# Causal attention in equal steps: a long row's rest and a short row share one of 17 steps of a head pair

## The chip, the cores and the metric

The kernel runs on one core of a Trainium2 chip. The metric is the device time of one execution in microseconds (us), as the median of several runs. One execution was also profiled; its trace gives the rows below. Engines: PE is TensorE's matmul, PEld its weight load, DVE is VectorE, ACT is ScalarE, POOL is GpSimd, SP is SyncE, whose queue issues all DMA transfers of this kernel in program order.

## The reference

A sandwich layer on x of 2 x 2048 x 1024 float32: layer norm, causal self-attention with 16 heads of 64, layer norm of its output and residual; then layer norm, a gated expert FFN of low rank, layer norm and residual.

```python
scores = jnp.einsum('bqhd,bkhd->bhqk', q, k) * inv_sqrt_hd
causal = jnp.triu(jnp.ones((S, S), dtype=bool), k=1)
scores = jnp.where(causal[None, None, :, :], -jnp.inf, scores)
probs = jax.nn.softmax(scores, axis=-1)
attn = jnp.einsum('bhqk,bkhd->bqhd', probs, v).reshape(B, S, D)
return attn @ wo.T + bo
...
x = x + _layernorm(_L0_attn_ref(_layernorm(x), wq, bq, wk, bk, wv, bv, wo, bo))
x = x + _layernorm(_L0_ffn_ref(_layernorm(x), ...))
```

## The kernel before, in words

All matmuls run on float16 high and low halves: three products (low x high, high x low, high x high) stand for one float32 product.

The attention phase goes over 16 head pairs (a batch and two neighbouring heads each; pairs 0 to 7 are batch 0). In a pair the 2048 queries are 16 row tiles of 128 ("rows"), row t against t + 1 key blocks of 128. A long row (t from 8 to 15) is cut in a first part of 8 blocks and a rest of t - 7 blocks, whose results are rescaled to a common maximum and added; a short row (t from 0 to 7) is one part of t + 1 blocks. A round is one long and one short row, `(15, 0)`, `(14, 1)` and so on, in three steps: first part, rest, short row. So a pair has 8 rounds and 24 steps of 1 to 8 blocks. A step has one task for each of the two heads.

What each engine does for a task:
- PE, `scores`: 6 matmuls for each piece of up to 512 key columns (both heads of a pair at once, on 64 rows of the array each) into one of three PSUM tiles `s_ps`. It waits until the exponential of the step before's first head has read its tile.
- DVE, `row_max`: adds the mask to the diagonal block, takes the row maximum, makes the exponential's bias.
- ACT, `exponentials`: the exponential into `probs` (ring of 24 blocks), then a copy to float16 into `hl` (ring of 40 blocks).
- POOL, `probs_low`: the low half into `hl`.
- SP, `transpose_probs`: a DMA transpose of both halves into `pt` (ring of 40 blocks); before it can be issued, the task that held its place must have been multiplied (`pv_done`).
- PE, `times_v`: 3 matmuls of 65 columns for each block into `o_ps`.

The order is written by hand: in step i of pair p every engine runs its function `body`. PE issues the scores of step i + 3 (`LAG`), then a share of a projection unit of the next pair (`project`; 12 units a pair, for q, k and v in four chunks of tokens each, two steps for each unit), then the products with V of step i. DVE reads out a finished round (`output_read`, `output_sum`), does `row_max` of step i + 3, evacuates a finished unit (`unit_full`), splits the weights of a coming pair in halves (`split_weight`, placed by `SPLITS`). ACT and POOL go alike. In pairs 0 to 6 the layer norm of batch 1 is made in the second step of each round (`NORM_STEPS`), and in pairs 6 and 7 its 16 tiles are transposed from DRAM into `arena` (`TURN_STEPS`: pair 6 steps 10 to 22, pair 7 steps 0 to 16, every second one). After four rounds the output rows are split in halves and stored (`rows_high`, `rows_low`, `store_rows`).

The last pair has no projection beside it. In its step 0 SP loads four blocks of the output projection's weights (L382) and all eleven other inputs of the finish (L384); the further four blocks (L387) follow in steps 5 to 8. ACT, DVE and POOL centre and split these weights (`wo_sum`, `center_wo`, `wo_high`, `wo_low`).

The finish phase (a block of its own, with a barrier ahead of it) goes over 32 tiles of 128 tokens: output projection of 48 matmuls (L1143 to L1145), norms, FFN.

Of the kernel before, what the change touches and what calls it, by code (L numbers as in the profile page):

```python
# [12 lines left out]
P = 128  # L13
B, S, D, H = 2, 2048, 1024, 16
HD = D // H
# [43 lines left out]


STEPS = rounds(range(QT // 2))
FIRST_STEPS = rounds(reversed(range(QT // 2)))
steps_of = lambda p: STEPS if p else FIRST_STEPS
NSTEP = len(STEPS)
N_ROUND = NSTEP // PER_ROUND
# [8 lines left out]
TASK_BLOCKS = [nb for p in range(PAIRS) for t, k0, nb, acc in steps_of(p) for h in range(2)]  # L74


def ring(capacity):

    at, before, live, pos = [], [], [], 0
    for n, nb in enumerate(TASK_BLOCKS):  # L80
# [28 lines left out]
STEPS_PER_UNIT = NSTEP // N_UNIT  # L109


last_step = lambda kind, m: STEPS_PER_UNIT * (1 + max(u for u, (n, c) in enumerate(UNITS[kind]) if n == m)) - 1
# [4 lines left out]
SPLITS["last"] = {}  # L117

# [3 lines left out]
FREE_STEPS = [(p, i) for p in range(PAIRS) for i in range(1, NSTEP, PER_ROUND)][1:]  # L122
# [10 lines left out]
TURN_STEPS = {"pre": {10 + 2 * i: i for i in range(7)}, "turn": {2 * i: 7 + i for i in range(9)}}  # L133
# [11 lines left out]
def units_ending(kind, i):  # L145
    return [i // STEPS_PER_UNIT] if UNITS[kind] and i >= 0 and i % STEPS_PER_UNIT == STEPS_PER_UNIT - 1 else []


def attend_phase(nc, x, w_pairs, mask_in, xn_scratch, o_scratch, arena, fin):
    with ExitStack() as ctx:  # L150
        sb = lambda name, shape, dt: ctx.enter_context(nc.sbuf_tensor(name, shape, dt))
        psum = lambda name: ctx.enter_context(nc.psum_tensor(name, [P, 512], F32))
# [38 lines left out]
        s_ps = [ctx.enter_context(nc.psum_tensor(f"s_ps{i}", [P, CHUNK * P], F32)) for i in range(S_RING)]  # L191
        o_ps, u_ps = psum("o_ps"), psum("u_ps")
# [100 lines left out]

        def probs_of(n):
            return probs[:, P_AT[n] * P:(P_AT[n] + TASK_BLOCKS[n]) * P]
# [19 lines left out]
        def _(sp):  # L315
# [23 lines left out]
            def store_rows(p, half):  # L339
# [3 lines left out]
                for which in range(2):  # L343
                    first = min(steps_of(p)[PER_ROUND * r + 2 * which][0] for r in range(4 * half, 4 * half + 4))
# [4 lines left out]
            def body(p, kind):  # L349
                for i in range(NSTEP):  # L350
# [6 lines left out]
                    for tile in norm_tiles(p, i - 1, 2):  # L357
# [15 lines left out]
                    if i == 14:  # L373
# [14 lines left out]
                    if kind == "last" and i == 20:  # L388
# [29 lines left out]
        def _(pe):  # L418
            def scores(p, i):
                t, k0, nb, acc = steps_of(p)[i]  # L420
                n = NTASK * p + 2 * i
                pe.wait_ge(unit_lo_done, units_before(p, [("q", t // 4)] + [("k", c) for c in range((k0 + nb + 3) // 4)]))
                if n >= S_RING - 1:
                    pe.wait_ge(exp_done, n + 2 - S_RING)
                rows, qk = slice(t * P, (t + 1) * P), nat[p % 2]
                q_hi, q_lo, k_hi, k_lo = range(4)
                for at in range(0, nb * P, 512):
                    end = min(nb * P, at + 512)
                    keys = slice(k0 * P + at, k0 * P + end)
                    for q, k in ((q_lo, k_hi), (q_hi, k_lo), (q_hi, k_hi)):  # L430
                        for h in range(2):
# [75 lines left out]
        def _(dve):  # L507
# [53 lines left out]
            def row_max(p, i):  # L561
# [8 lines left out]
                for h in range(2):  # L570
                    n = NTASK * p + 2 * i + h
                    if diagonal:
                        dve.wait_ge(mask_done, masked + h + 1)
# [955 lines left out]
```

## Time and profile before

| | |
|---|---|
| median of 3 runs | 2527.53 us (2524.58 to 2529.49) |
| the profiled execution | 2525.55 us |
| its span, first to last instruction | 2523.8 us |
| before the first product with V | 116.4 us |
| pairs 0 to 14 | 116.4 to 1922.7 us |
| last pair, to the last product with V | 1922.7 to 2057.8 us |
| finish | 2057.8 to 2523.8 us |
| mean granted TensorE clock | 0.968 |

A share of busy time over the span mixes these stages. The bounds of the pairs are the starts of their first product with V in the trace. How to read a row is said at its group; "idle before us <-releaser" is the time an engine sat idle before these instructions, and what ended it.

### The profile page before, as it was taken

How to read it: one execution, taken by the hardware profiler on the slowest of the kernel's cores; microseconds unless marked ns; L12 is line 12 of the kernel's file. 1: busy time of each engine (PE TensorE's matmuls, PEld its weight loads, DVE VectorE, ACT ScalarE, POOL GpSimd, SP SyncE). 2: the span in 40 equal slices, each digit the busy share in tenths (PEclk: the TensorE clock that was granted, in tenths of full speed). 3: DMA queues.
4: the chain of work that ended last, by engine and by line, in shares of the span. 5: the costliest groups of instructions: out<-in, count | busy, mean ns of one | idle time of the engine just before them, and what ended most of it. 6: DMA issues, size and time to landing. Idle time of an engine off the chain costs nothing. (4 is left out here: it accounts for less than half of the span.)

```text
span 2523.8 us, 71940 instructions
## 1 busy us (share of the span) xinstructions
PE 2313.6 (92%) x28626; PEld 1451.6 (58%) x28626; DVE 1734.3 (69%) x4154; ACT 1782.1 (71%) x2579; POOL 1714.0 (68%) x1519
## 2 busy tenths in 40 slices
PE   4899999999999997899999999999997559999995
PEld 2466666575757655556675757666664334544452
DVE  8577877787777755567666776767665635777776
ACT  3477877777877866577778777877777835666664
POOL 4488888888878876678888788888887832222221
PEclk9999999999999999999999999999998779999997
DMA  9699999999999999999999999999999975666663
GB/s 240 128 199 192 202 191 194 199 194 189 202 192 199 189 185 188 194 167 193 173 184 183 171 184 178 190 169 189 169 173 193 174 147 134 167 153 159 161 164 84
DMA packets 1433645, 450.16 MB, mean 178 GB/s; under 512 B 1410240, under 2 KB 1411536, under 8 KB 1433312
## 3 DMA queue, kind: packets, MB, share of 16 engines
q1 hardware_dynamic: 1433312, 445.57, 95.7%
q8 instruction: 228, 3.74, 0.6%
q14 instruction: 105, 0.86, 0.1%
HBM read 67.95 MB, written 41.94 MB: 44 GB/s over the span
## 5 line engine op out<-in xcount | busy, mean ns | idle before, releaser
L848 POOL TENSOR_TENSOR hl<-probs,hl 128x1024 f16<-128x1024 f32 (+7 forms) x768 | 1229.3, 1612 | 366.3 <-ACT hl L731 365.5
L726 ACT ACTIVATE probs<-s_ps,exp_bias 128x1024 f32<-128x1024 f32 (+7 forms) x768 | 655.6, 854 | 386.3 <-DVE exp_bias L577 382.3
L574 DVE TENSOR_REDUCE neg_max<-s_ps 128x1 f32<-128x1024 f32 (+7 forms) x768 | 694.6, 904 | 68.9 <-PE s_ps L432 68.8
L731 ACT ACTIVATE hl<-probs 128x1024 f16<-128x1024 f32 (+7 forms) x768 | 620.5, 808 | 47.8 <-DMA pt<-hl 24.1
L450 PE MATMUL o_ps<-v,pt 128*128 128x65 f16 x4352 | 451.1, 194 | 60.4 <-DMA pt<-hl 50.7
L432 PE MATMUL s_ps<-nat 64*128 64x512 f16 (+3 forms) x3840 | 433.6, 354 | 65.2 <-ACT probs L726 60.3
L450 PEld LDWEIGHTS o_ps<-v,pt 128*128 128x128 f16 x4352 | 405.0, 97 | 107.6 <-issue 40.4
L451 PE MATMUL o_ps<-v,pt 128*128 128x65 f16 x4352 | 451.3, 195 | 0.0
L452 PE MATMUL o_ps<-v,pt 128*128 128x65 f16 x4352 | 449.4, 193 | 0.0
L479 PE MATMUL u_ps<-arena,w 128*128 128x512 f16 x1008 | 389.8, 387 | 40.2 <-DMA arena<-hl 35.3
L451 PEld LDWEIGHTS o_ps<-v,pt 128*128 128x128 f16 x4352 | 404.3, 98 | 27.8 <-issue 0.3
L452 PEld LDWEIGHTS o_ps<-v,pt 128*128 128x128 f16 x4352 | 405.0, 99 | 0.0
L480 PE MATMUL u_ps<-arena,w 128*128 128x512 f16 x1008 | 386.8, 384 | 0.0
L481 PE MATMUL u_ps<-arena,w 128*128 128x512 f16 x1008 | 386.4, 383 | 0.0
L475 PE MATMUL u_ps<-w,arena 128*128 128x128 f16 x1984 | 340.2, 220 | 0.7 <-DVE full L558 0.7
L476 PE MATMUL u_ps<-w,arena 128*128 128x128 f16 x1984 | 338.9, 219 | 0.0
L477 PE MATMUL u_ps<-w,arena 128*128 128x128 f16 x1984 | 338.9, 219 | 0.0
L569 DVE TENSOR_TENSOR s_ps<-s_ps,mask 128x128 f32<-128x128 f32 x512 | 126.5, 292 | 285.6 <-PE s_ps L432 285.1
L432 PEld LDWEIGHTS s_ps<-nat 64*128 64x128 f16 x3840 | 161.3, 95 | 211.1 <-issue 76.4
L479 PEld LDWEIGHTS u_ps<-arena,w 128*128 128x128 f16 x1008 | 99.0, 98 | 212.6 <-issue 115.8
L475 PEld LDWEIGHTS u_ps<-w,arena 128*128 128x128 f16 x1984 | 194.0, 98 | 38.3 <-issue 36.8
L1143 PE MATMUL proj_ps<-arena,w 128*128 128x512 f16 x512 | 195.0, 381 | 7.8 <-PEq L150 7.8
(150 smaller groups left out, 3690.4 us busy)
## 6 DMA issues: line engine op xcount, KB each, us to landing
w_raw<-in_w_pairs SPq DMA_DIRECT2D x48, 576.0 KB, 4.7
o_scratch<-o_hl SPq DMA_DIRECT2D x128, 128.0 KB, 2.6
out<-result SPq DMA_DIRECT2D x32, 512.0 KB, 2.9
x_in<-in_x SPq DMA_DIRECT2D x27, 512.0 KB, 5.1
pt<-hl SPq DMA_TRANSPOSE x768, 4.5
nat<-in_x SPq DMA_DIRECT2D x16, 512.0 KB, 4.8
xn_scratch<-xn SPq DMA_DIRECT2D x16, 512.0 KB, 4.2
xn<-in_x SPq DMA_DIRECT2D x11, 512.0 KB, 3.9
```

Source lines behind the costliest of these rows:

```text
L432: mm = nc.tensor.matmul(s_ps[(n + h) % S_RING][:, at:end], qk[HEADS[h], q, rows], qk[HEADS[h], k, keys], start=(q == q_lo), stop=(q == q_h ...
L450: nc.tensor.matmul(dst, lo, v_hi, start=(first and k == 0), stop=False)
L451: nc.tensor.matmul(dst, hi, v_lo, start=False, stop=False)
L452: mm = nc.tensor.matmul(dst, hi, v_hi, start=False, stop=(last and k == nb - 1))
L475: nc.tensor.matmul(dst, xt[:, 1, k, toks], hi[:, k, :], start=first, stop=False)
L479: nc.tensor.matmul(bank, lo[:, k, :], xt[:, 0, k, toks], start=first, stop=False)
L480: nc.tensor.matmul(bank, hi[:, k, :], xt[:, 1, k, toks], start=False, stop=False)
L481: mm = nc.tensor.matmul(bank, hi[:, k, :], xt[:, 0, k, toks], start=False, stop=last)
L574: nc.vector.tensor_reduce(neg_max[:, r, acc, h:h + 1], s_ps[n % S_RING][:, 0:nb * P], AX_X, ALU.max, negate=True).then_inc(max_done, 1)
L726: nc.scalar.activation(probs_of(n), s_ps[n % S_RING][:, 0:nb * P], ACT.Exp, bias=exp_bias[:, r, acc, h:h + 1], scale=SOFTMAX_SCALE).then_i ...
L731: nc.scalar.activation(hl_of(n, 0), probs_of(n), ACT.Copy).then_inc(p_hi_done, 1)
L848: nc.gpsimd.tensor_tensor(hl_of(n, 1), probs_of(n), hl_of(n, 0), ALU.subtract).then_inc(p_lo_done, 1)
```

## The change

The rounds are paired otherwise, so that a long row's rest and the short row of its round make 8 blocks together: `(14, 0)` has a rest of 7 and a short row of 1, `(8, 6)` of 1 and 7. They share one step, with one task for each head; only `(15, 7)` keeps three steps. A pair has 17 steps of 8 blocks each. In a shared step masks, maxima, biases and exponentials are made part by part; copy, low half, transpose and products with V run over the whole task. The place of a short row in the output scratch follows a table (`slot_of`).

Projection units take one or two steps each (`UNIT_STEPS`), the splits and the transposes of x have new steps, norm work stands in the step that closes a round. In the last pair the loads are dealt out over steps 0 to 6, two small matrices are laid out by partition on the host (a transfer of long rows), and the output projection of tile 0 (`project_half`) is issued at the end of the attention block, ahead of the barrier; PSUM tiles are shared by both phases for that.

```diff
-PER_ROUND = 3
-def rounds(order):
-    steps = []
-    for i in order:
-        t_long, t_short = QT - 1 - i, i
-        steps += [(t_long, 0, CHUNK, 0), (t_long, CHUNK, t_long + 1 - CHUNK, 1), (t_short, 0, t_short + 1, 2)]
-    return steps
+ROUNDS = [(14, 0), (13, 1), (12, 2), (15, 7), (11, 3), (10, 4), (9, 5), (8, 6)]
+FIRST_ROUNDS = [(8, 6), (9, 5), (10, 4), (11, 3), (12, 2), (13, 1), (14, 0), (15, 7)]
+SHORT_SLOTS = [3, 4, 5, 6, 0, 1, 2, 7]
+slot_of = lambda t: t if t >= CHUNK else SHORT_SLOTS.index(t)
+Step = namedtuple("Step", "round parts blocks opens closes")
+def steps(rows):
+    out = []
+    for r, (t_long, t_short) in enumerate(rows):
+        first, rest, short = (t_long, 0, CHUNK, 0), (t_long, CHUNK, t_long + 1 - CHUNK, 1), (t_short, 0, t_short + 1, 2)
+        shared = [[rest, short]] if rest[2] + short[2] <= CHUNK else [[rest], [short]]
+        tasks = [[first]] + shared
+        out += [Step(r, parts, sum(part[2] for part in parts), i == 0, i == len(tasks) - 1)
+                for i, parts in enumerate(tasks)]
+    return out
...
-STEPS_PER_UNIT = NSTEP // N_UNIT
+UNIT_STEPS = {"first": [1, 1, 2, 2, 1, 1, 1, 2, 1, 2, 1, 2], "mid": [1, 1, 1, 2, 1, 2, 1, 2, 1, 2, 1, 2],
+              "pre": [1, 1, 1, 2, 1, 1, 1, 2, 2, 1, 2, 2], "turn": [1, 1, 1, 2, 1, 1, 1, 2, 2, 1, 2, 2], "last": []}
-SPLITS = {kind: {4: "q", last_step(kind, "k") + 1: "k",
-                 max(last_step(kind, "k") + 4, last_step(kind, "v") + 1): "v"} for kind in ("mid", "pre", "turn")}
-SPLITS["first"] = {1: "v", 5: "q"} | {i: m for i, m in SPLITS["mid"].items() if m != "q"}
+SPLITS = {"mid": {3: "q", 6: "k", 14: "v"}, "pre": {3: "q", 13: "k", 16: "v"}, "turn": {3: "q", 13: "k", 16: "v"}}
+SPLITS["first"] = {1: "v", 4: "q", 7: "k", 14: "v"}
-FREE_STEPS = [(p, i) for p in range(PAIRS) for i in range(1, NSTEP, PER_ROUND)][1:]
+FREE_STEPS = [(p, i) for p in range(PAIRS) for i, step in enumerate(steps_of(p)) if step.closes][1:]
-TURN_STEPS = {"pre": {10 + 2 * i: i for i in range(7)}, "turn": {2 * i: 7 + i for i in range(9)}}
+TURN_STEPS = {"pre": {i: n for n, i in enumerate((6, 8, 9, 11, 12, 14, 15))},
+              "turn": {i: 7 + n for n, i in enumerate((0, 1, 3, 4, 5, 7, 8, 9, 10))}}
...
-                        for k in range(4):
-                            sp.dma_start(wo_raw[k], fin["w_view"][k]).then_inc(wo_loaded[k], 16)
-                        for tile, source in fin["loads"]:
+                    if kind == "last" and i < 4:
+                        sp.dma_start(wo_raw[i], fin["w_view"][i]).then_inc(wo_loaded[i], 16)
+                    if kind == "last" and i >= 1:
+                        for tile, source in fin["loads"][2 * i - 2:2 * i]:
                             sp.dma_start(tile, source).then_inc(fin_loaded, 16)
...
             def exponentials(p, i, h):
...
+                at = 0
+                for t, k0, nb, acc in step.parts:
+                    cols = slice(at, at + nb * P)
+                    last = nc.scalar.activation(probs_of(n)[:, cols], s_ps[n % S_RING][:, cols], ACT.Exp,
+                                                bias=exp_bias[:, step.round, acc, h:h + 1], scale=SOFTMAX_SCALE)
+                    at += nb * P
+                last.then_inc(exp_done, 1)
...
             pairs(body)
+            pe.wait_ge(exp_done, NTASK * PAIRS)
+            pe.wait_ge(wo_lo_done, KT)
+            pe.wait_ge(fin["ot_loaded"][0], 16)
+            for h in range(2):
+                project_half(nc, fin, 0, h)
```

## Rows read from the trace of the kernel before

**Rows 1.** The page: span, and busy time of each engine over the span.

```profile
span 2523.8 us, 71940 instructions
...
PE 2313.6 (92%) x28626; PEld 1451.6 (58%) x28626; DVE 1734.3 (69%) x4154; ACT 1782.1 (71%) x2579; POOL 1714.0 (68%) x1519
```

**Rows 2.** Busy time by stretch: pairs 0, 7, 10, 14, 15, and the finish.

```profile
core 0: us, PE busy (x) PEld busy (x) DVE busy (x) ACT busy (x) POOL busy (x), PEclk, DMA share, GB/s
...
116.40:236.80 120.40, 115.36 (x1633) 76.15 (x1632) 92.48 (x208) 93.46 (x132) 99.09 (x76) 1.00 1.11 198
...
970.40:1113.00 142.60, 124.19 (x1634) 78.87 (x1633) 78.68 (x194) 90.74 (x129) 95.79 (x70) 0.94 1.04 181
...
1346.10:1462.00 115.90, 115.00 (x1634) 75.87 (x1633) 80.11 (x195) 90.78 (x130) 96.61 (x70) 1.00 1.06 181
...
1809.50:1922.70 113.20, 112.42 (x1621) 74.65 (x1620) 73.63 (x188) 88.07 (x127) 92.44 (x67) 1.00 1.06 170
1922.70:2057.80 135.10, 70.84 (x1016) 47.93 (x1014) 77.31 (x173) 95.30 (x136) 94.58 (x64) 0.71 0.91 181
...
2101.00:2523.80 422.80, 388.73 (x2356) 198.35 (x2354) 305.47 (x856) 260.15 (x434) 91.79 (x307) 0.96 0.59 148
```

**Rows 3.** Waits of TensorE in pairs 0 to 7: total us, times, longest.

```profile
PE o_ps L450 <- DMA pt<-hl: 27.0, 25, 3.2
PE s_ps L432 <- ACT probs L726: 18.9, 27, 2.5
PE u_ps L479 <- DMA arena<-xn_scratch: 4.2, 1, 4.2
```

**Rows 4.** Timeline of TensorE over one step of pair 10: start, us, operation.

```profile
1448.80 0.19 PE L451 MATMUL o_ps<-v,pt 128*128 128x65 f16 x1
1448.83 0.19 PE L452 MATMUL o_ps<-v,pt 128*128 128x65 f16 x1
1448.95 1.47 PE L432 MATMUL s_ps<-nat 64*128 64x512 f16 x12
1450.35 0.39 PE L479 MATMUL u_ps<-arena,w 128*128 128x512 f16 x1
...
1452.95 0.19 PE L450 MATMUL o_ps<-v,pt 128*128 128x65 f16 x1
```

**Rows 5.** Timeline of VectorE after the scores of a masked eight-block step.

```profile
1450.46 0.50 DVE L569 TENSOR_TENSOR s_ps<-s_ps,mask 128x128 f32<-128x128 f32 x2 [0.20 <-PE s_ps L432]
1450.87 1.22 DVE L574 TENSOR_REDUCE neg_max<-s_ps 128x1 f32<-128x1024 f32 x1
```

**Rows 6.** Groups by shape in pair 10: count, busy us, mean ns, idle before.

```profile
L574 DVE TENSOR_REDUCE neg_max<-s_ps 128x1 f32<-128x1024 f32 x21 | 25.6, 1217 | 3.4 <-PE s_ps L432 3.4
...
L726 ACT ACTIVATE probs<-s_ps,exp_bias 128x1024 f32<-128x1024 f32 x21 | 23.2, 1105 | 17.0 <-DVE exp_bias L577 17.0
...
L731 ACT ACTIVATE hl<-probs 128x1024 f16<-128x1024 f32 x20 | 21.1, 1057 | 0.6
...
L726 ACT ACTIVATE probs<-s_ps,exp_bias 128x128 f32<-128x128 f32 x4 | 1.4, 350 | 0.0
```

**Rows 7.** The low half of the split weights, whole run: ns min/median/max.

```profile
L542 DVE SCALAR_TENSOR_TENSOR w<-w_raw,w x48: 1209/1300/3161, 11.2 to 1834.6; 128x1024 f16<-128x1024 f32 x48
```

**Rows 8.** SyncE's transposes of probabilities, whole run: issue ns min/median/max, and landing.

```profile
L337 SPq DMA_TRANSPOSE pt<-hl x768: 1188/1867/4313, 99.8 to 2050.9; - x192
...
DMA to landing us min/median/max: 2.3/4.5/7.9
```

**Rows 9.** Waits in the last pair: total us, times, longest.

```profile
PE s_ps L432 <- ACT probs L726: 35.0, 16, 6.0
...
PE o_ps L450 <- DMA pt<-hl: 23.3, 9, 9.0
...
ACT arena L755 <- DMA nat<-in_w_o: 10.0, 5, 6.1
```

**Rows 10.** Timeline at the start of the finish.

```profile
2065.60 0.59 PE L1143 MATMUL proj_ps<-arena,w 128*128 128x512 f16 x1 [7.82 <-PEq L150]
```

More of the change, by code:

```diff
@@ L1 @@
 import math
+from collections import namedtuple
 from contextlib import ExitStack
@@ L72 @@
 P_BLOCKS, HL_BLOCKS, PT_BLOCKS, T_RING = 24, 40, 40, 16
-TASK_BLOCKS = [nb for p in range(PAIRS) for t, k0, nb, acc in steps_of(p) for h in range(2)]
+TASK_BLOCKS = [step.blocks for p in range(PAIRS) for step in steps_of(p) for h in range(2)]
 def ring(capacity):
@@ L292, in dst_of, with first_step, half_done @@
             return nat[p % 2][:, 2 * WHICH[m] + part, c * 512:(c + 1) * 512]
+        def first_step(p, r):
+            return sum(step.round < r for step in steps_of(p))
+        def half_done(p):
+            return first_step(p, N_ROUND // 2) + 1
         def probs_of(n):
@@ L343, in store_rows @@
                 for which in range(2):
-                    first = min(steps_of(p)[PER_ROUND * r + 2 * which][0] for r in range(4 * half, 4 * half + 4))
+                    first = min(slot_of(rounds_of(p)[r][which]) for r in range(4 * half, 4 * half + 4))
                     for part in range(2):
@@ L426, in scores @@
                 q_hi, q_lo, k_hi, k_lo = range(4)
[L427 to L431, printed above, removed]
-                            mm = nc.tensor.matmul(s_ps[(n + h) % S_RING][:, at:end], qk[HEADS[h], q, rows],
-                                                  qk[HEADS[h], k, keys], start=(q == q_lo), stop=(q == q_hi and k == k_hi))
+                at = 0
@@ L434, in scores @@
                 mm.then_inc(s_done, 2)
             def times_v(p, i, h):
-                t, k0, nb, acc = steps_of(p)[i]
-                n, first, last = NTASK * p + 2 * i + h, i % PER_ROUND == 0 and h == 0, i % PER_ROUND == 2 and h == 1
-                done = N_ROUND * p + i // PER_ROUND
+                step, n = steps_of(p)[i], NTASK * p + 2 * i + h
+                done = N_ROUND * p + step.round
                 if h == 0:
-                    pe.wait_ge(unit_lo_done, units_before(p, [("v", c) for c in range((k0 + nb + 3) // 4)]))
+                    for t, k0, nb, acc in step.parts:
+                        pe.wait_ge(unit_lo_done, units_before(p, [("v", c) for c in range((k0 + nb + 3) // 4)]))
@@ L442, in times_v @@
                 pe.wait_ge(pt_done[n % T_RING], 16 * (n // T_RING + 1))
-                if first and done >= 1:
+                if step.opens and h == 0 and done >= 1:
                     pe.wait_ge(part_done, done)
                     pe.wait_ge(short_done, done)
-                for k in range(nb):
-                    hi, lo = pt_of(n)[:, k, :], pt_of(n)[:, nb + k, :]
-                    v_hi, v_lo = (v[p % 2][:, k0 + k, part, h, 0:HD + 1] for part in range(2))
+                blocks = [(k0 + k, acc) for t, k0, nb, acc in step.parts for k in range(nb)]
@@ L449, in times_v @@
+                for at, (k, acc) in enumerate(blocks):
+                    hi, lo = pt_of(n)[:, at, :], pt_of(n)[:, step.blocks + at, :]
+                    v_hi, v_lo = (v[p % 2][:, k, part, h, 0:HD + 1] for part in range(2))
                     dst = o_acc[:, acc, h, :]
-                    nc.tensor.matmul(dst, lo, v_hi, start=(first and k == 0), stop=False)
+                    first = step.opens and h == 0 and at == 0
+                    last = step.closes and h == 1 and at == step.blocks - 1
+                    nc.tensor.matmul(dst, lo, v_hi, start=first, stop=False)
@@ L570, in row_max @@
[L570 to L578 removed]
+                step, n = steps_of(p)[i], NTASK * p + 2 * i
@@ new lines, in row_max @@
+                dve.wait_ge(s_done, n + 2)
+                places = []
+                for part in step.parts:
+                    first = places[-1][2] if places else 0
+                    places.append((part, first, first + part[2] * P))
+                masked = 2 * (QT * p + sum(is_diagonal(part) for step in steps_of(p)[:i] for part in step.parts))
+                for h in range(2):
+                    for part, first, end in places:
+                        if is_diagonal(part):
+                            last = s_ps[(n + h) % S_RING][:, end - P:end]
+                            nc.vector.tensor_tensor(last, last, mask[:], ALU.add).then_inc(mask_done, 1)
@@ L1179, in step @@
             def step(m, has):
-                if has(0):
+                if has(0) and m >= 1:
                     project(m, 0)
```

172 lines of the change are left out of this document (98 added, 74 removed).

## The prediction

> **What bounds the kernel now.** I read first the page's totals, then a table of one stretch per head pair (from the first to the next pair's first product with V), then the waits of TensorE, then one step as a timeline. The totals [rows 1] show TensorE busy 92% of the span, the other three engines near 70%. The table [rows 2] splits that. In the middle pairs (8 to 13; the one shown is pair 10, the others lie at 115.7 to 117.2) TensorE is busy 115.0 of 115.9 us at full granted clock: they are bound by TensorE. The pairs 0 to 5 last 120.4, 117.7, 122.9, 119.2, 120.7 and 124.2, pair 6 128.9, pair 7 142.6, with TensorE's busy time hardly higher: there it waits. The last pair, which has no projection beside it, takes 135.1 with TensorE busy 70.8. Over pairs 0 to 7 the waits [rows 3] name the late partners: the transposed probabilities (27.0 us), the exponentials (18.9) and one transpose of x (4.2); the rest of the 69 us above 8 x 115.9 is granted clock below 1.00 in pairs 6 and 7 [rows 2]. So three things can be won: switches inside a full TensorE, waits in pairs 0 to 7, and the last pair with what joins it to the finish.
>
> **The same work in fewer steps.** A pair has 136 blocks for each head, before and after: 24 steps of 1 to 8 blocks become 17 steps of 8. The score matmuls stay 240 a pair (a shared step is cut at the same 512 columns, and the pieces of 4, 3, 2 and 1 blocks are the same in number), products with V stay 816, projections 12 units. Masks, row maxima and exponentials go by part, so they stay too; copies to f16, low halves on GpSimd and transposes go by task and fall from 48 to 34 a pair.
>
> TensorE's own time. In one step [rows 4] the products with V follow each other at 0.03 us, but the first score comes 0.12 after the last product: 0.09 lost. The 12 scores take 1.40 until the projection starts; at the projection's own pace (12 matmuls in 2.60, 0.217 each) six pairs of concurrent scores would take 1.30: 0.10 lost. A step thus costs 0.19 beside its columns, and 7 steps less save 1.3 us a pair, 21 us in 16. This is the one gain that no cover can hide where TensorE is the bound. Built up, a pair after is 17 x 1.40 for scores, 12 units of 5.2 to 5.3 (63), 816 x 0.03 plus 17 x 0.09 for products (26.3): 113. The same sum for before gives 114.7, so 1.2 of its 115.9 are small waits after steps of one or two blocks.
> The Trainium skill ("TensorEngine Tiling (Array Packing)", Tiling Modes) says that a change of tiling mode drains the array, and "TensorE: Matmul & The Clock Gate" (Step-by-step) puts a drain at about 128 cycles, 0.053 us at 2.4 GHz. As an estimate by that page alone, two switches in 112 steps would be 12 us; the row's 0.19 includes what it does not, and the row decides.
>
> What could take its place in these pairs. The scores of step s+1 need the exponential of step s's first head. In a shared step that chain is: four masks before the first maximum (0.41 for two in [rows 5], so 0.83), two maxima over 8 blocks together (1.22 for one [rows 6]; the second instruction adds between 0 and ACT's 0.24, I take 0.15), two small bias operations 0.3, two exponentials (1.11 plus a fixed part of 0.24, from 350 ns at one block and 1105 at eight [rows 6]): 3.85 us. TensorE covers it, in the shortest step (half a unit), with 2.60 + 48 x 0.03 + 0.12 = 4.15 [rows 4]; with a whole unit, 6.7. Cover 0.3 us in 4 of 8 shared steps of a pair: thin. If it fails, each 0.1 us costs 6 us over 15 pairs. A second cover: the split of q's weights now comes at step 3 on ACT and 4 on VectorE and its unit at step 5 (before: 4, 5 and 8). VectorE must first do masks, maxima, the sum of the last round and a unit's evacuation, some 6 us of a 5.6 us step, then 1.2 to 3.2 for the split [rows 7]; the projection may start late by 0 to 1.9 us, I take 0.5 a pair. Of ACT's and GpSimd's own loads, 14 copies less of 0.24 fixed part are 3.4 us a pair less, from 90.8 and 96.6 [rows 2]: neither bounds. With 0.5 for the split and 1.1 for other bunching I take 114.6 for a middle pair (113 to 116): 6 pairs give 696.5 - 687.6 = 9, pair 14 1.
>
> **Pairs 0 to 7.** SyncE issues all transfers in order, and a transpose keeps it 1.19 us even for one block, 1.87 in the median [rows 8]; 14 issues less a pair free at least 17 us of a queue that has 48 of them, 90 us. What the eight-block ones cost is the rate of the DMA engines, and the bytes don't change. Pair 7 moves 142.6 x 181 = 25.8 MB [rows 2], 9 transposes of x among it. Without the short issues the queue should reach what the stretches of long transfers show, between the 181 of pair 7 and the 198 of pair 0 as lower ends and some 220 if the gaps behind short issues close: 117 us. The 9 transposes lie in 11 steps of 17 instead of 17 of 24, about as dense; the last one is issued two steps of 6.7 us before its unit instead of two of 4.8. I take 119.5 for pair 7 (114 to 136), 117 for pair 6, 116.5 for pair 0, 115.3 for pairs 1 to 5. The norm work, moved to the closing steps, stays 48 pieces in the same pairs and falls beside row maxima of one part without masks. Together 725.1 - 693 = 32, 12 and 23.
> The Trainium skill ("DMA: Bandwidth & Descriptors", Latency and other measured facts) gives DMA transposes 261 GB/s in one layout. By an estimate with that figure pair 7 would need 99 us of transfer and be bound by TensorE, 5 us below what I take. No row of before shows a stretch at that rate.
>
> **Last pair and finish.** ACT is busy 95.3 of 135.1 us [rows 2]. The waits [rows 9] show TensorE behind transposed probabilities (23.3) and exponentials (35.0), ACT behind weights of the output projection (10.0): SyncE issues four of these and eleven other loads in one run at step 0, with the probabilities' transposes behind them. The change deals them out over steps 0 to 6 and lays two of them out by partition. ACT needs 95.3 - 3.4 = 92, and from the last scores on some 12 us follow in which ACT is idle: 104 is the floor. I leave 11 of the waits: 115, a gain of 20 (0 to 30). What comes next in line is ACT itself, 4.8 us of exponentials and copies a step plus 2.3 for a block of weights.
> TensorE then waits 7.82 us [rows 10] for the block's end before the first output projection. That projection (48 matmuls, over 10 us) now stands ahead of the barrier, beside the last rows' evacuation; a barrier of some 2.5 us follows it. The finish is bound by TensorE (388.7 of 422.8 in the rest of the table), so the start counts in full: 5.5 (0 to 7).
>
> **Sum.** 9 + 1 + 32 + 12 + 23 + 20 + 5.5 = 102.5. The profiled execution took 2525.55 us (span 2523.8), 2 below the median of 2527.53: forecast 2423.
>
> **The rivals.**
> 1. All covers hold and the queue is free: 114 in each pair (98 less), last pair 110, finish 7: 2396. For it: the middle pairs of before already run within 1.2 us of their sum. Against: the thin covers. 0.15.
> 2. The chain of the shared step outlasts its cover: VectorE reaches it late (output of the last round, norm, evacuation) by 0.8 us in 4 steps of 15 pairs: 48 us back, 2471. For it: VectorE's chain has four masks ahead of the first maximum. It would show as waits of scores for exponentials in middle pairs. 0.16.
> 3. The DMA rate stays at 190 GB/s: pair 7 at 136, pair 6 at 123, some 5 in pairs 0 to 5: 2423 + 16 + 6 + 5 = 2450. 0.10.
> 4. The rings decide, and the kernel is slower: 40 blocks of transposed probabilities and of their copies hold 5 tasks of 8 instead of 7 of mixed size. The second head's transpose of step s can't be issued before the first head's product of step s-2; from there to its use are two steps less 0.7, 10.4 us at the shortest. Landing takes 4.5 in the median and 7.9 at the longest [rows 8], with up to one issue ahead of it. So some 4 us are left as a rule and 0.6 at worst. It would be slower than before once every one of the 272 steps lost 0.38 us, that is with landings of over 9 us throughout: 2540. 0.03.
> 5. The last pair isn't smoother (the loads, each behind a transpose that waits for a product, come late to ACT): 20 back, 2443. 0.06.
> The forecast itself: 0.50. In every case but the fourth it is faster. A measurement of this kernel can tell about 0.2%, 5 us, from no change: faster 0.95, same 0.02, slower 0.03. The range 2394 to 2470 leaves out the fourth, half of the second and some of the first.
>
> **What would show it.** Transposes 544, ACT 2355 and GpSimd 1295 instructions, TensorE's 28626 unchanged. Right: middle pairs at 114 to 115 with busy TensorE; pair 7 below 125; the wait for transposed probabilities in pairs 0 to 7 below 8 us; the gap before the first output projection gone, with one of 2 to 3 us behind it. Wrong: scores waiting for exponentials by over 1 us a pair (rival 2), the projection waiting for the split weights, or ACT's copies waiting for transposes in middle pairs (rival 4).

## The result, and the profile after

The changed kernel takes 2612.36 us (median of 4, 2609.91 to 2615.06) against 2526.16 for the kernel before, a ratio of 1.034 (1.0322 to 1.0358): slower by 86 us, where 2423 was forecast. The profiled execution took 2613.59 us.

The page of the changed kernel, span and busy time, to lay beside [rows 1]:

```profile
span 2611.8 us, 70598 instructions
...
PE 2291.2 (88%) x28626; PEld 1449.2 (55%) x28626; DVE 1701.4 (65%) x4154; ACT 1726.7 (66%) x2355; POOL 1682.1 (64%) x1295
```

Every engine has less work, as foreseen, and the span is 88 us longer. The stretches of pairs 0, 7, 10, 14 and 15, to lay beside [rows 2]:

```profile
core 0: us, PE busy (x) PEld busy (x) DVE busy (x) ACT busy (x) POOL busy (x), PEclk, DMA share, GB/s
121.40:242.20 120.80, 113.64 (x1633) 75.99 (x1632) 87.58 (x209) 89.48 (x117) 96.69 (x61) 1.00 1.05 186
1014.40:1150.60 136.20, 118.48 (x1632) 77.93 (x1633) 82.55 (x203) 87.99 (x116) 94.82 (x56) 0.96 1.13 197
1400.50:1526.00 125.50, 115.72 (x1633) 76.46 (x1632) 77.15 (x195) 87.34 (x116) 94.03 (x57) 0.99 0.95 166
1901.20:2022.30 121.10, 108.83 (x1609) 73.58 (x1608) 72.58 (x184) 85.20 (x113) 91.10 (x56) 1.00 0.94 161
2022.30:2154.70 132.40, 61.52 (x997) 44.32 (x998) 68.93 (x169) 88.96 (x120) 88.05 (x48) 0.75 0.95 189
```

Where the 88 us lie, by the starts of the first products with V:

| stretch | before | after | difference | forecast difference |
|---|---|---|---|---|
| before the first product | 116.4 | 121.4 | +5.0 | 0 |
| pairs 0 to 5 | 725.1 | 759.3 | +34.2 | -32 |
| pair 6 | 128.9 | 133.7 | +4.8 | -12 |
| pair 7 | 142.6 | 136.2 | -6.4 | -23 |
| pairs 8 to 13 | 696.5 | 750.6 | +54.1 | -9 |
| pair 14 | 113.2 | 121.1 | +7.9 | -1 |
| last pair | 135.1 | 132.4 | -2.7 | -20 |
| finish | 466.0 | 457.1 | -8.9 | -5.5 |

The first line is scatter and no effect of the change that could be told: the profiled executions below, whose edits leave this stretch alone, lie between 116.1 and 121.4. The loss is 8 to 10 us in every middle pair, where TensorE was full before, so its cause is new. The waits of the changed kernel over pairs 0 to 14 (total us, times, longest), chosen from the view:

```profile
DVE o_part L649 <- ACT factor L798: 176.0, 50, 9.5
...
DVE o_rows L655 <- POOL o_hl L928: 109.0, 29, 5.2
...
PE s_ps L467 <- ACT probs L783: 86.9, 62, 1.9
...
PE o_ps L490 <- DVE o_rows L655: 41.0, 34, 3.5
...
PE u_ps L519 <- DVE w L588: 39.6, 15, 2.8
```

The same view of the kernel before:

```profile
PE o_ps L450 <- DMA pt<-hl: 27.5, 26, 3.2
PE s_ps L432 <- ACT probs L726: 25.3, 42, 2.5
DVE o_rows L601 <- POOL o_hl L869: 22.8, 15, 2.5
...
DVE o_part L595 <- ACT factor L739: 4.8, 3, 3.5
```

So TensorE no longer waits for a transpose of probabilities at all (27.5 before), but VectorE, which hardly waited for ScalarE or GpSimd before (4.8 and 22.8 us; its other waits were for TensorE's results), stands still for 285 us behind ScalarE's factors of a long row (L798) and behind GpSimd's low half of the output rows (L928). TensorE's three waits above follow from it. One place in pair 10 shows how; first ScalarE, then VectorE, then TensorE (start, us, operation, idle before):

```profile
1426.18 1.06 ACT L790 ACTIVATE hl<-probs 128x1024 f16<-128x1024 f32 x1
1427.15 1.04 ACT L763 ACTIVATE w<-w_raw 128x1024 f16<-128x1024 f32 x1
1428.09 0.47 ACT L798 ACTIVATE factor<-exp_bias,bias_min 128x2 f32<-128x2 f32 x2
1431.23 1.11 ACT L783 ACTIVATE probs<-s_ps,exp_bias 128x1024 f32<-128x1024 f32 x1 [2.67 <-DVE exp_bias L631]
```

```profile
1428.65 0.43 DVE L649 TENSOR_TENSOR o_part<-o_ps,factor 128x260 f32<-128x260 f32 x1 [5.58 <-ACT factor L798]
...
1429.19 0.29 DVE L655 TENSOR_TENSOR o_rows<-o_ps,inv_short 128x128 f32<-128x128 f32 x1
...
1429.79 1.22 DVE L626 TENSOR_REDUCE neg_max<-s_ps 128x1 f32<-128x1024 f32 x1
...
1433.75 2.97 DVE L588 SCALAR_TENSOR_TENSOR w<-w_raw,w 128x1024 f16<-128x1024 f32 x1
```

```profile
1429.63 0.19 PE L490 MATMUL o_ps<-v,pt 128*128 128x65 f16 x1 [1.08 <-DVE o_rows L655]
...
1432.49 1.47 PE L467 MATMUL s_ps<-nat 64*128 64x512 f16 x12 [1.25 <-ACT probs L783]
1436.77 0.39 PE L519 MATMUL u_ps<-arena,w 128*128 128x512 f16 x1 [2.81 <-DVE w L588]
```

In the round's second step ScalarE makes the factors last: behind both heads' exponentials and copies, which belong to a step three further on, and behind the split of q. VectorE's next instruction is the readout, and its row maxima come behind that, so it idles 5.58 us with finished scores in front of it. Then three waits of TensorE: the opening product for the readout of `o_ps`, the scores for the late exponential, the projection for the split of q, which VectorE reaches last. Over pair 10 these three kinds are all of TensorE's idle time:

```profile
PE s_ps L467 <- ACT probs L783: 5.4, 4, 1.9
...
PE u_ps L519 <- DVE w L588: 2.8, 1, 2.8
...
PE o_ps L490 <- DVE o_rows L655: 1.6, 2, 1.1
```

Together 9.8 = 125.5 - 115.7. The same pair without these stops (the last kernel below) takes 113.1 us, all of them busy; so 2.6 us more of TensorE's busy time are the other part of a loss of 12.4. About 1.7 of them are clock: right behind the wait of 2.81 the granted clock is 0.57 (of 2.4 GHz, mostly the 1.2 level) for 4 us, and the matmuls from 1437.21 to 1440.84 come up to 0.43 apart instead of 0.22. The remaining 0.9 fits the way busy time is counted: seven waits stand in this pair, and the last matmul ahead of each counts with its whole length (0.19 for a product with V) and not with its 0.03 of pace, an estimate of 1 us. The first row is ahead of the waits, the second behind the longest:

```profile
1425.80:1428.50 2.70, 2.70 (x14) 1.07 (x12) 0.00 (x0) 2.67 (x5) 2.70 (x2) 1.00 0.86 160
1436.70:1440.70 4.00, 3.93 (x11) 1.49 (x12) 3.05 (x8) 2.14 (x3) 2.35 (x2) 0.57 0.82 152
```

### The profile page after: what moved, and what is told of

It reads as the page before. It is cut to its first block and busy times, and to the rows that moved or that the text cites. A ratio compares the mean times of both kernels' runs of the same rounds, so it can differ in the third digit from the quotient of the medians.

```text
span 2611.8 us, 70598 instructions
## 1 busy us (share of the span) xinstructions
PE 2291.2 (88%) x28626; PEld 1449.2 (55%) x28626; DVE 1701.4 (65%) x4154; ACT 1726.7 (66%) x2355; POOL 1682.1 (64%) x1295
## 5 line engine op out<-in xcount | busy, mean ns | idle before, releaser
L907 POOL TENSOR_TENSOR hl<-probs,hl 128x1024 f16<-128x1024 f32 x544 | 1194.9, 2202 | 484.3 <-ACT hl L790 479.6
L783 ACT ACTIVATE probs<-s_ps,exp_bias 128x1024 f32<-128x1024 f32 (+7 forms) x768 | 633.5, 854 | 577.8 <-DVE exp_bias L631 576.6
L626 DVE TENSOR_REDUCE neg_max<-s_ps 128x1 f32<-128x1024 f32 (+7 forms) x768 | 676.1, 905 | 77.5 <-PE s_ps L467 77.5
L790 ACT ACTIVATE hl<-probs 128x1024 f16<-128x1024 f32 x544 | 575.0, 1057 | 20.2 <-DMA pt<-hl 2.9
L467 PE MATMUL s_ps<-nat 64*128 64x512 f16 (+3 forms) x3840 | 411.6, 352 | 125.7 <-ACT probs L783 122.7
L490 PE MATMUL o_ps<-v,pt 128*128 128x65 f16 x4352 | 432.9, 194 | 79.3 <-DVE o_rows L655 69.2
L519 PE MATMUL u_ps<-arena,w 128*128 128x512 f16 x1008 | 391.9, 389 | 77.3 <-DVE w L588 39.6
L491 PE MATMUL o_ps<-v,pt 128*128 128x65 f16 x4352 | 433.3, 195 | 0.0
L492 PE MATMUL o_ps<-v,pt 128*128 128x65 f16 x4352 | 432.3, 193 | 0.0
L515 PE MATMUL u_ps<-w,arena 128*128 128x128 f16 x1984 | 338.1, 219 | 3.1 <-DVE w L588 2.9
L467 PEld LDWEIGHTS s_ps<-nat 64*128 64x128 f16 x3840 | 168.5, 95 | 263.0 <-issue 142.4
L519 PEld LDWEIGHTS u_ps<-arena,w 128*128 128x128 f16 x1008 | 99.7, 99 | 244.8 <-issue 101.0
L649 DVE TENSOR_TENSOR o_part<-o_ps,factor 128x260 f32<-128x260 f32 x128 | 54.5, 426 | 260.4 <-ACT factor L798 187.2
L515 PEld LDWEIGHTS u_ps<-w,arena 128*128 128x128 f16 x1984 | 193.9, 98 | 42.3 <-issue 38.6
L1061 PE MATMUL s_ps<-arena,w 128*128 128x512 f16 x512 | 194.8, 380 | 0.0
```

Source lines behind the costliest of these rows:

```text
L467: mm = nc.tensor.matmul(s_ps[(n + h) % S_RING][:, at:end], qk[HEADS[h], q, rows], qk[HEADS[h], k, keys], start=(q == q_lo), stop=(q == q_h ...
L490: nc.tensor.matmul(dst, lo, v_hi, start=first, stop=False)
L491: nc.tensor.matmul(dst, hi, v_lo, start=False, stop=False)
L492: mm = nc.tensor.matmul(dst, hi, v_hi, start=False, stop=last)
L515: nc.tensor.matmul(dst, xt[:, 1, k, toks], hi[:, k, :], start=first, stop=False)
L519: nc.tensor.matmul(bank, lo[:, k, :], xt[:, 0, k, toks], start=first, stop=False)
```

## The experiments

All are timed beside the kernel before on the same chip (medians of 2524.86 to 2526.68 us). The stretches and waits given are those of each run's one profiled execution. "The three mends" are those of the first four runs.

**The factors first.** ScalarE makes the factors ahead of the exponentials of the step; nothing else moves.

```diff
                     step = step_of(p, i, kind)
+                    if i and steps_of(p)[i - 1].opens:
+                        chunk_factors(p, steps_of(p)[i].round)
                     if step:
                         exponentials(*step, 0)
...
-                    if i and steps_of(p)[i - 1].opens:
-                        chunk_factors(p, steps_of(p)[i].round)
```

> The changed kernel, but ACT makes a round's rescaling factors ahead of the exponentials of its closing step, not behind them. Theory A (the readout of a round waits for these factors, since a round now has two steps and not three): VectorE's wait of 176 us for factors over pairs 0 to 14 falls below 30, TensorE's waits for exponentials (86.9) and for the readout (41.0) fall by half or more together, and the kernel gains 40 to 70 us, to 2545 to 2570. Rival B (the chain of masks and maxima in a shared step outlasts its cover, rival 2 of the prediction): VectorE's wait for factors goes, but scores go on waiting for exponentials, and the gain is under 15 us.

Measured: 2526.98 us (8 runs), ratio 1.0003 (0.9991 to 1.0015): 85 us less than the change, from moving two short instructions a round. Pairs 8 to 13 fall from 125 to 116.8. VectorE's wait for factors is gone from pairs 0 to 14, and part of it has moved on:

```profile
DVE o_rows L655 <- POOL o_hl L928: 138.6, 29, 6.6
```

That was 109.0: the next stop in VectorE's order. The gain is above the expectation: a late VectorE had also made the split of q late (TensorE's wait for `w` at L519 falls from 39.6 to 12.9 us with it).

**q split one step earlier.**

```diff
-SPLITS = {"mid": {3: "q", 6: "k", 14: "v"}, "pre": {3: "q", 13: "k", 16: "v"}, "turn": {3: "q", 13: "k", 16: "v"}}
+SPLITS = {"mid": {2: "q", 6: "k", 14: "v"}, "pre": {2: "q", 13: "k", 16: "v"}, "turn": {2: "q", 13: "k", 16: "v"}}
-SPLITS["first"] = {1: "v", 4: "q", 7: "k", 14: "v"}
+SPLITS["first"] = {1: "v", 3: "q", 7: "k", 14: "v"}
```

> The changed kernel, but the split of q's weights is placed one step earlier (step 2 of a pair, step 3 of the first). Theory C (the projection starts late behind this split; TensorE's waits for it are 42.5 us over pairs 0 to 14, foreseen at 0.5 us a pair): the waits go, and the kernel gains 30 to 43 us, to 2570 to 2582. Rival: another wait (exponentials, readout) takes their place in the same steps; gain under 10 us.

Measured: 2583.83 us, ratio 1.0235 (1.0212 to 1.0259): 28.5 less than the change, just short of the 30 to 43 expected; pairs 8 to 13 at 121 to 124. TensorE's waits for the split weights fall from 42.5 to 1.9 us, so not all of them became time. Most of the loss stays (VectorE waits 137.9 us for factors), so the split is a part, not the cause.

**A second place for the short rows.** The output of a short row alternates between two places, so that the readout need not wait for GpSimd's low half of the previous four rounds.

```diff
-        o_rows = sb("o_rows", [P, 2, 4, 2, HD], F32)
+        o_rows = sb("o_rows", [P, 3, 4, 2, HD], F32)
...
-                if n >= 4:
-                    dve.wait_ge(o_lo_done, n // 4)
-                nc.vector.tensor_tensor(o_rows[:, 1, ...
+                if n >= 8:
+                    dve.wait_ge(o_lo_done, n // 4 - 1)
+                nc.vector.tensor_tensor(o_rows[:, n // 4 % 2 * 2, ...
```

> The changed kernel, but the short rows' output has two places in SBUF, so that VectorE's readout of the first round of a half doesn't wait for GpSimd's low half of the half before. Theory A (second part): VectorE's wait of 109 us for that low half goes; one such wait of about 4 us a half pair delays the row maxima and then TensorE by some 1 to 2 us in 30 places: gain 20 to 50 us, to 2562 to 2592. Rival B: gain under 10 us, since VectorE's chain is late anyway.

Measured: 2553.94 us, ratio 1.0117 (1.0086 to 1.0148): 58 less than the change, above the expectation; pairs 8 to 13 at 119.5 to 121.8.

**All three.**

> The changed kernel with all three edits: factors first, q's split one step earlier, short rows' output twice. Theory A with C: a middle pair comes to 114 to 117 us, as the sum of TensorE's own work (113) says, and the kernel to 2430 to 2475, faster than before by 2 to 4%. Rival B: the scores go on waiting for exponentials in shared steps by over 2 us a pair, and the kernel stays above 2510.

Measured: 2487.15 us (2483.26 to 2491.16), ratio 0.9858 (0.9839 to 0.9877), 125 less than the change, but above the 2430 to 2475 expected: the middle pairs do even better than was expected for them, while pairs 0 to 5, pair 7 and the last pair have stops of their own, which the later runs take up. The single gains add to 172, more than 125. That fits stops that stand one behind the other in VectorE's order, where taking one away also shortens or bares the next, as the first run shows. Pairs 8 to 13 now last 113.2 to 113.3, the prediction's sum of TensorE's own work. Pair 10 of this kernel, then its pair 7 and its last pair:

```profile
1333.60:1447.00 113.40, 113.40 (x1634) 75.89 (x1633) 76.32 (x194) 87.81 (x116) 93.26 (x57) 1.00 1.09 184
968.90:1107.30 138.40, 119.69 (x1634) 77.42 (x1633) 77.10 (x194) 88.53 (x116) 93.63 (x57) 0.93 1.09 192
1894.50:2024.70 130.20, 60.99 (x999) 42.13 (x998) 73.98 (x169) 90.26 (x122) 90.38 (x49) 0.74 1.01 196
```

TensorE is busy in all of pair 10, with the four masks and two maxima of the shared steps as in the changed kernel. So the rival of a shared step whose chain outlasts its cover falls.

**The converse, in the old schedule.** In the kernel before, with its three steps a round, the factors are put where the change has them: one step ahead of the readout, behind the exponentials.

```diff
-                    if i % PER_ROUND == 1:
+                    if i % PER_ROUND == 2:
                         chunk_factors(p, i // PER_ROUND)
```

> The old schedule of three steps a round, with one thing moved: ScalarE makes the two factors of a long row one step later, behind the exponentials of the round's third step, as far ahead of VectorE's readout as they stand in the changed kernel. Theory A (the factors, queued behind two exponentials that belong to later work, hold up VectorE's readout, and in VectorE's order the next row maxima behind it): slower than the kernel before, by 20 to 90 us, VectorE's readout waits for ScalarE's factors by over 3 us a pair in the middle pairs, which go from 115.9 to 118 to 121 us. Rival (the old order has other slack, and the stall comes of the shared steps themselves, twice the number of small instructions): within 5 us of the kernel before.

Measured: 2681.91 us, ratio 1.0626 (1.0603 to 1.0649): 155 us slower, beyond the expectation's 90. The waits over pairs 0 to 14:

```profile
DVE o_part L595 <- ACT factor L739: 322.4, 106, 8.3
...
PE s_ps L432 <- ACT probs L726: 118.3, 94, 5.0
```

The middle pairs go from 115.9 to between 128 and 129.6. One step of slack made the whole difference, without a shared step in the kernel. The loss is larger than the 85 us above in about the ratio of VectorE's waits for factors (322.4 us in 106 stops against 176.0 in 50). This and the first run settle the main cause.

**The norm's transfers between two transposes.** On the kernel with the three mends VectorE still waits 50.5 us for the load of x in pairs 0 to 5. `store_norm` is the store of xn and the next load of x.

```diff
+            def transpose_probs(p, i, norm=()):
                 for h in range(2):
+                    if h:
+                        for tile in norm:
+                            store_norm(tile)
```

> The kernel with all three mends, with the norm's store and its next load of x on SyncE's queue moved ahead by one transpose (between the two heads' transposes of a step, not behind the second). Theory L (in pairs 0 to 6 the load comes late because the second transpose waits in SyncE's queue for a place in the ring): VectorE's wait for x falls from 50 us to below 20, pairs 0 to 5 go from 121.5 to 115 to 118 each, 20 to 35 us faster than the kernel with three mends (2487). Rival R (the transfers of these pairs, 23 to 24.5 MB each, are bound by the rate of 190 to 203 GB/s): pairs 0 to 5 within 1 us of 121.5 on the mean, total within 5 us of 2487.

Measured: 2454.07 us (2447.83 to 2456.59), ratio 0.9715 (0.9692 to 0.9738), 33 less. Pairs 0 to 5 take 698.3 instead of 729.1 us, all but the first 114.6 to 116.5. VectorE's wait in this kernel, and the six pairs in one stretch, then the same stretch with the three mends alone:

```profile
DVE stats_a L567 <- DMA x_in<-in_x: 18.6, 9, 4.7
```

```profile
118.00:816.30 698.30, 682.32 (x9793) 455.44 (x9792) 529.82 (x1244) 540.07 (x705) 589.64 (x366) 1.00 1.12 201
```

```profile
116.30:845.40 729.10, 690.67 (x9793) 458.69 (x9792) 526.25 (x1245) 541.21 (x706) 592.34 (x367) 0.98 1.06 194
```

The rival of a bound by the rate falls for these pairs: the same bytes went at 201 GB/s once the load left in time. The second transpose of a step waits for a place in a ring of five tasks, and the load had stood behind it.

**The weights of the last pair.** With the three mends the last pair still takes 130.2 us. ScalarE's longest wait there, and SyncE's queue ahead of it:

```profile
1956.53 1.06 ACT L814 ACTIVATE arena<-nat 128x1024 f16<-128x1024 f32 x1 [10.08 <-DMA nat<-in_w_o]
```

```profile
1948.03 2.45 SPq L366 DMA_TRANSPOSE pt<-hl  x1
1950.53 0.81 SPq L415 DMA_DIRECT2D arena<-in_rank  x1
1951.40 0.42 SPq L415 DMA_DIRECT2D arena<-in_center  x1
1951.87 0.43 SPq L418 DMA_DIRECT2D nat<-in_w_o  x1
```

Weight block 4 leaves at 1951.87 and lands 4.6 us later, while ScalarE's exponentials of the next step stand behind it. In the run the loads of blocks 4 to 7 stand ahead of their step's transposes, and the engines work on these blocks two steps later:

```diff
+WO_AT = [2, 3, 4, 5, 8, 9, 10, 11]
...
-                    if kind == "last" and 2 <= i < 2 + KT:
-                        wo_sum(i - 2)
+                    for k in range(KT):
+                        if kind == "last" and i == WO_AT[k]:
+                            wo_sum(k)
```

> The kernel with all three mends; in the last pair the loads of the output projection's weight blocks 4 to 7 stand ahead of their step's two transposes, and ScalarE, VectorE and GpSimd work on them two steps later. Theory W (in the last pair all engines stand still because ScalarE, in order, waits for a weight block that was issued too late behind transposes, 10.1 us at step 6 alone): ScalarE's wait for weights falls from 21 us to below 10, the last pair from 130.2 to 115 to 120. Rival R (the last pair moves 25.5 MB at 196 GB/s, 130 us: the rate of the transfers bounds it): the last pair stays within 3 us of 130, the idle time turns up at the wait for transposed probabilities.

Measured: 2480.16 us, ratio 0.9819 (0.979 to 0.9848). The last pair falls to 121.4 us, ScalarE's wait for weights from 21.4 to 7.9. That is between the two expectations: the pair is 8.8 us shorter, where theory W gave 10 to 15; the 25.5 MB moved at 210 GB/s, so 196 had been no bound.

**The loads in one run again.**

```diff
-                    if kind == "last" and i < 4:
-                        sp.dma_start(wo_raw[i], fin["w_view"][i]).then_inc(wo_loaded[i], 16)
-                    if kind == "last" and i >= 1:
-                        for tile, source in fin["loads"][2 * i - 2:2 * i]:
+                    if kind == "last" and i == 0:
+                        for k in range(4):
+                            sp.dma_start(wo_raw[k], fin["w_view"][k]).then_inc(wo_loaded[k], 16)
+                        for tile, source in fin["loads"]:
```

> The kernel with all three mends; in the last pair the first four weight blocks and all eleven other loads are issued in one run at step 0 again, as in the kernel before, instead of dealt out over steps 0 to 6. It sizes this part of the change alone. By the prediction (dealing them out is most of a gain of 20 us) the last pair goes from 130.2 to 145 to 150. By what the traces of the changed kernels suggest (the stop behind block 4, issued late among dealt-out loads, takes the place of the stop at step 0): within 4 us of 130.2, with ScalarE's longest wait for a weight block below 7 us and longer waits for probabilities near the pair's start.

Measured: 2482.53 us, ratio 0.9825 (0.98 to 0.985); the last pair 125.9, 4.3 less than with the loads dealt out. Both expectations miss, the second narrowly: ScalarE's longest wait for weights is 7.9 us, not below 7. Dealing the loads out gains nothing by itself.

**Fewer bytes in pair 7.** With the three mends pair 7 still takes 138.3 us, 17.2 of them waits of TensorE for x in `arena`. Here eight of the nine transposes of x fetch 2 of 16 blocks; the other blocks keep batch 0's values.

```diff
+                        if n < 8:
+                            transpose_x(LN_TILES + n, tile, xn_scratch[tile])
+                        else:
+                            sp.dma_start_transpose(
+                                xt.rearrange("p l k n -> p (l k) n")[:, 0:2, tile * P:tile * P + P],
+                                xn_scratch[tile][:, 0:2 * P]).then_inc(xt_done[n % 4], 16)
```

> The kernel with all three mends; of the nine transposes of x in pair 7, eight (tiles 8 to 15 of batch 1) fetch 2 of their 16 blocks, the other blocks of these tiles keep the values of batch 0, so that 3.7 MB less are moved in the same order with the same waits. Theory R (pair 7 is bound by the rate of the transfers, 26.6 MB at 192 GB/s): pair 7 falls from 138.3 by 15 to 20 us to 118 to 123, the waits for arena (17.2 us) go, nothing else changes: total 2467 to 2472. Rival Q (the transposes of x are issued too late in SyncE's order, whatever their size): pair 7 falls by less than 6 us.

Measured: 2470.64 us, ratio 0.9787 (0.9763 to 0.981), 16.5 less, nearly all in pair 7:

```profile
971.40:1093.50 122.10, 115.18 (x1633) 76.39 (x1632) 77.04 (x194) 89.26 (x117) 92.99 (x57) 0.99 1.11 188
```

The order and the waits in the program are the same; 3.7 MB less took 16 us away, and the rate stayed near (188 for 192). The mends and orders of the other runs leave pair 7 at 136 to 140. So pair 7 is bound by how much its transfers move and not by a late place of x in the order, and the waits for `arena` are mostly a symptom (6.1 us of them stayed). Whether the DMA engines' rate or SyncE's time to issue binds was not separated: the shorter transposes also took 11.5 us less to issue (all issues of the pair take 126.9 us with the three mends and 115.4 here), and 192 GB/s is not the most that a pair reached (204 in pair 5 of the same kernel).

**The two gains together, then the finish's loads behind the last transposes.**

> The kernel with all three mends, with the norm's transfers between the two transposes and with the later work on the weight blocks together (the edits of the two single runs). If the two gains lie in different stretches and add: 2487 - 33 - 8 = 2446 (2440 to 2452), pairs 1 to 5 at 115 to 116.5, the last pair at 121. Rival: the queue, fuller in pairs 0 to 5, hands its load on to later pairs; then over 2455.

Measured: 2447.69 us (2441.48 to 2453.58), ratio 0.9688 (0.9661 to 0.9715). They add (2446 expected), within the scatter of 12 us; pairs 1 to 5 spread more than expected, 113.5 to 119.8.

```diff
-                    if kind == "last" and i == 12:
+                    if kind == "last" and i == 13:
                         for m in range(2):
                             fin["load_o"](sp, m)
                             fin["load_x"](sp, m)
```

> The same kernel as the one beside it, with one thing more: the first two transposes of the attention's output and the two loads of x for the finish stand behind the last transposes of probabilities, not one step ahead of them. Theory: they hold the last step's probabilities back by 7.6 us on SyncE's queue (TensorE waits 8.6 us for them); the last pair falls from 121.4 to 114 to 117 and 3 us of it are lost again at the start of the finish, 3 to 6 us faster than the kernel beside it. Rival (the finish then waits for what was put off): within 2 us of it, or slower.

Measured: 2442.41 us (2437.68 to 2445.26, 5 runs), ratio 0.9663 (0.9639 to 0.9686): 3.4% faster than the kernel before and 170 us faster than the change. Against the kernel beside it that is 5.3 us in the medians, as expected, but the ranges overlap; the traces show the last pair at 112.2 instead of 122.0, below the 114 to 117 expected, and the finish 2.1 longer. Its last pair and its pair 10:

```profile
1872.20:1984.40 112.20, 64.30 (x998) 43.79 (x996) 77.73 (x169) 89.85 (x122) 91.41 (x49) 0.75 1.12 213
1424.70:1537.80 113.10, 113.10 (x1633) 75.59 (x1632) 76.29 (x194) 87.59 (x116) 93.11 (x57) 1.00 1.10 185
```

## Why the prediction was wrong

The failed step is a term that the prediction put at nothing without a reason: VectorE's wait for the inputs of the readout. It followed the chain of the scores (masks, maxima, exponential) and counted its cover; of the readout it counted only VectorE's own time. "With 0.5 for the split and 1.1 for other bunching I take 114.6 for a middle pair" is where the wait should have stood; the middle pairs measured 125.1 on the mean. Before, the factors were made in the second step of three and read at the next round's start, with a whole step between; with two steps a round the same line of code leaves none, and the wait went from 4.8 to 176.0 us over fifteen pairs. The wait for GpSimd's low half went from 22.8 to 109.0. The factors are the largest part: 85 us by the first run, 125 together with the two other mends.

- **The switches of a step**: the sum is right. 0.19 us a step gave 113 for a pair; with the stops gone the middle pairs take 113.2, TensorE busy throughout. How much of the 2.7 us below the kernel before are switches and how much are its small waits was not measured apart. By their own terms the products come to 26.0 and not 26.3, and the sum for before to 114.1 and not 114.7.
- **The cover of the shared step** (3.85 under 4.15): it holds in the middle pairs; the rival built on it is refuted by the kernel with three mends. Its sign, scores waiting over 1 us a pair, did come (5.4 in pair 10), by another cause.
- **The split of q**: foreseen, mis-sized. 0.5 us a pair was taken of a range of 0 to 1.9; TensorE waited 42.5 us in 15 pairs (39.6 at L519, 2.9 at L515), 2.8 each. The range ended too low since VectorE itself came late, and the split of q took 2.97 us in nearly every pair, while GpSimd's second subtraction beside it took 3.09 instead of 2.13. Mending it alone gave 28.5.
- **Pairs 0 to 7, the waits for transposes**: right, 27.0 us [rows 3] to none, and to 5.3 with the three mends, where TensorE no longer comes late itself. Of what it called clock in pairs 6 and 7 (19 us) the granted clocks of 0.97 and 0.94 give about 12. **The freed queue**: wrong. Issuing 34 transposes in pair 10 takes SyncE 90.2 us instead of 94.7 for 48, summed over their records: 4.5 us less, not 17. The first row is pair 10 of before, the second that of the kernel with three mends:

```profile
L337 SPq DMA_TRANSPOSE pt<-hl x49: 1196/1787/4268, 1342.8 to 1458.6; - x49
```

```profile
L366 SPq DMA_TRANSPOSE pt<-hl x35: 1318/2672/4875, 1332.0 to 1445.7; - x35
```

  (The views count one more at the edge of the stretch.) So 1.19 us for each transpose left out [rows 8] was not there to be saved. In the kernel before, the shortest issue took 1.19 us for one block and 1.32 for eight, the medians were 1.59 and 2.37; fewer and longer ones held SyncE nearly as long for the same bytes, and what holds it beyond the shortest time stays open. So pair 7 was mis-sized: 119.5 forecast (25.8 MB in that time are 216 GB/s), 136.2 measured. That is the third rival's 136, in part by luck: the stretch moved 26.8 MB, at 197 and not at 190. The Trainium skill ("DMA: Bandwidth & Descriptors", Latency and other measured facts) gives DMA transposes in one layout 261 GB/s; the highest stretch of a pair in any run here is 213. In pairs 0 to 5 the forecast of 693 us was wrong by 66, for the stops and for late loads of x: with both mended they take 698.3. The moved norm work was costed at nothing; beside row maxima it is, but its transfers on SyncE's queue were not looked at.
- **Last pair**: wrong, 2.7 us instead of 20. Of TensorE's waits of [rows 9] the one for transposed probabilities fell from 23.3 to 9.9 us and the one for exponentials stayed (35.1), while the one for VectorE's readout rose from 5.9 to 28.2, and ScalarE's for weights from 10.0 to 15.5. The step "deals them out over steps 0 to 6" looked at the first four weight blocks, not at block 4, whose work follows its late load. With that and the finish's loads moved the pair takes 112.2 against the 115 forecast: the size could be had, but by orders that the change does not have. The fifth rival named this.
- **Finish**: right in kind, 8.9 us instead of 5.5. The gap of 7.82 us [rows 10] is gone, and the barrier costs TensorE 0.33 us, not 2.5, because the other engines' last work now lies under the projection (12.0 us, part of it at the lower clock). The first instruction behind the barrier:

```profile
2166.84 2.01 PE L1257 MATMUL o_ps<-arena 128*16 128x136 f32 x16 [0.33 <-PEq L173]
```

- **The fourth rival** (rings of five tasks) had the only slower case, and was not what happened: ScalarE waited for a transpose's place 2.9 us in the whole run. But the second transpose's wait for its ring did hold the loads of x.

The best kernel's profiled time stands 22 us above the forecast: pair 7 18.6, pairs 0 to 6 15.5, the start 5.0, less 8.4 in pairs 8 to 13, 4.2 in pair 14, 2.8 in the last and 1.4 in the finish. So the sum comes near a kernel whose other lines have been moved with the steps, with errors of both signs; for this one it left out what the new step count does to them. The chance of 0.03 for slower had no basis in a list of the waits that cross a round's border. What stays open: how the 125 us split among the three stops (they aren't additive), what of pair 7 is rate and what is issuing, and the 6 us and more above 113 that pair 0 keeps in every run.

## What to carry to other kernels

When a schedule gets fewer, longer steps, list for each engine every instruction that waits for another engine and count how many steps lie between the two, before and after: a hand-off that had a whole step of slack turns into a stop, and in an in-order engine all that stands behind it stops too. A wait of 5 us in the profile before is no proof that there is slack left. And loads that share a queue with transposes belong ahead of the one that waits for its ring.

## What the runs showed of the hardware

- A VectorE split of a weight and a GpSimd subtraction lengthen each other where they overlap, and the one that began first keeps its time. In pair 10 a GpSimd subtraction began at 1433.51 and took its usual 2.13 us; the split of q began inside it, at 1433.75, and took 2.97; the next subtraction began inside the split, at 1435.60, and took 3.09. The splits of k and v, begun while GpSimd stood still, took 1.22, and the subtraction that began 0.40 us into the split of k at 1456.59 took 2.81. The Trainium skill ("SBUF — State Buffer", Who interferes with whom) says that a VectorE operation with both inputs in SBUF contends with GpSimd's reads; the trace agrees here.
- A wait of 2.81 us, behind one of 1.08 and one of 1.25, was followed by 4 us at a granted clock of 0.57; about 1.7 of the 12.4 us that the stops cost this pair were clock, not waiting. Two waits of 1.86 us later in the pair, 13 us apart, were followed by a clock of 1.00.
- The transfers, by number 98% in packets under 512 bytes, ran at up to 213 GB/s over a stretch of 112 us (the last pair), and the rate there rose from 196 when the other engines stood still less: a rate seen in a profile can be what was asked for and no bound. It takes a run with fewer bytes, as for pair 7, to show that the transfers bind.
